# Gated cross-attention walks: order of VectorE's inverse and first addition, and of four maximum products on TensorE

## The chip, the cores and the metric

The program runs on one core of one Trainium2 chip. A core has TensorE (matmuls; PE in the profile, with its weight loads as PEld), VectorE (DVE), ScalarE (ACT), GpSimd (POOL) and SyncE (SP, which issues the DMAs here). Each engine works through its own instructions in order, and semaphores tie the engines together. The metric is the device time of one execution in microseconds (us).

## The reference

Four layers on x (16 sequences of 56 tokens, 256 features) with a context of 1500 rows of 128 features for each sequence. The first is self attention, cross attention and a gated feed-forward, the second a cross attention with a memory gate. The third and fourth are alike, and only their attention is touched here:

```
q = layernorm(x) @ Wq * scale                    # 16 heads of 64
k, v = split(media @ Wkv)                        # media: the context
sim = einsum('bhid,bhjd->bhij', q, k)
sim = where(media_mask[:, None, None, :], sim, neg_inf)
attn = softmax(sim)
x = x + tanh(attn_gate) * (attn @ v merged over heads @ Wo)
x = x + tanh(ff_gate) * (gelu(layernorm(x) @ W1) @ W2)
```

The mask handed in is true only for context positions beyond a sequence's length, so that `where` leaves no more than the last 375 of a sequence's 1500 rows: one chunk. The kernel's code has a second path for sequences with more than one chunk (`several`), which these inputs do not take.

## The kernel before

For each of the two gated layers (`l` 0 and 1) a walk over the batch handles one sequence after the other: B = 16 walks, written out one by one in the path taken. Queries are folded with the key weights, so that scores are products against the context itself: 896 columns (16 heads x 56 tokens) by 375 context rows. Walk b does two things at once.

It finishes sequence b from turned scores. `turned(u)`, u = 0 to 5, is a set of four matmuls (L2395 to L2398) for a third of the 375 rows and a half of the 896 columns; three multiply queries and context in split precision, the fourth subtracts the maxima by way of a diagonal matrix. ScalarE takes the exponential of each (`exps`, L1174, tile WA), and `values(u)` (L2403) multiplies it with the context into PSUM banks 5 and 6. VectorE adds the three thirds of the exponentials in `add_tiles` (L1727, the first addition) and `add_last` (L1733, the last addition).

It prepares sequence b + 1. `behind(j)`, j = 0 to 7, calls `maxima` (product at L2375) for one pair of heads into bank j % 2; `masked_maximum` on VectorE (L1710) adds the mask and takes the row maximum. In the trace it is two records, CUSTOM_DVE_ANT_0 and DVE_READ_ACCUMULATOR2_ANT. A product j waits until maximum j - 2 has read its bank (`x2_rowmax`). After the eighth maximum GpSimd builds the diagonal matrix (`diagonal`, L812, tile XN), for which `turned(0)` of the next walk waits. GpSimd then prepares a later context (`keys`, L803, L805, L807).

The denominators belong to the sequence before: in walk b, `denominators` on TensorE (L2411) multiplies the added exponentials of sequence b - 1 with ones into bank 7. VectorE copies them out (`denominators`, L1717) and inverts them in two halves (`invert(b, 0)` and `invert(b, 1)`, both L1723). The first exponential of a walk waits for the last addition of the walk before (`x2_dsum`), since it overwrites what that reads; the first addition waits for the fourth exponential, the last for the sixth.

The order on each engine is the order in which the code of `batch` (VectorE), `step` (TensorE, ScalarE) is written.

Of the kernel before, what the change touches and what calls it, by code (L numbers as in the profile page):

```python
# [198 lines left out]
def build(nc, a, out):  # L199

    ctx = ExitStack()
    with ctx:
# [1019 lines left out]
        def _(dve):  # L1222
# [250 lines left out]
            def invert(b):  # L1473

                dve.wait_ge(sem("z_one_each"), b + 1)
                V.reciprocal(z_few[:, 1, :], z_few[:, 1, :]).then_inc(sem("z_inverted"), 1)
# [218 lines left out]
            for l in range(2):  # L1695
                queries(l, 0, {0: lambda: centre("nq", l, 1), 3: lambda: inverse_root("nq", l, 1, 0),
                               4: lambda: inverse_root("nq", l, 1, 1), 5: lambda: scale("nq", l, 1, 0, 1)})
                queries(l, 1, {})

                def maximum(b, p, j):  # L1700
                    wait_at(dve, "x2_scores", PAIRS * (l * B + b) + j + 1)
                    V.tensor_reduce(y_max[p][0:PR, j:j + 1], bank[j % 2][0:PR, 0:CK], AX_X, ALU.max)\
                        .then_inc(sem("x2_rowmax"), 1)

                def masked_maximum(b, s, j):

                    if j == 0:
                        dve.wait_ge(sem(f"x2_mask{s}"), 16 * (B // SLOTS * l + b // SLOTS + 1 - (l + 1) * (s == 0)))
                    dve.wait_ge(sem("x2_scores"), PAIRS * (l * B + b) + j + 1)
                    V.tensor_tensor_reduce(y_masked[0:PR, j % 2, 0:CK], bank[j % 2][0:PR, 0:CK], y_mask[0:PR, s, 0:CK], 1.0, -3e38,  # L1710
                                           ALU.add, ALU.max, y_max[s % 2][0:PR, j:j + 1])\
                        .then_inc(sem("x2_rowmax"), 1)

                def denominators(k):

                    wait_at(dve, "x2_dn", l * (B + 1) + k + 1)
                    V.tensor_copy(y_den[:, bass.ds(k, 1), :].rearrange("p b n -> p (b n)"), bank[7][:, 0:HALF])\  # L1717
                        .then_inc(sem("x2_den"), 1)
                    wait_at(dve, "x2_den", l * (B + 1) + k + 2)

                def invert(k, g):
                    part = y_den[:, bass.ds(k, 1), g * HALF // 2:(g + 1) * HALF // 2].rearrange("p b n -> p (b n)")
                    V.reciprocal(part, part).then_inc(sem("x2_inverted"), 1)  # L1723

                def add_tiles(b):
                    wait_at(dve, "x2_expd", PARTS * (l * B + b) + 4 + 3)
                    V.tensor_tensor(y_sum[0:TK, :], y_pT[0][0:TK, :], y_pT[1][0:TK, :], ALU.add)\  # L1727
                        .then_inc(sem("x2_dsum"), 1)

                def add_last(b):  # L1730
                    wait_at(dve, "x2_expd", PARTS * (l * B + b) + PARTS + 3)
                    wait_at(dve, "x2_dsum", 2 * (l * B + b) + 3)
                    V.tensor_tensor(y_sum[0:TK, :], y_sum[0:TK, :], y_pT[2][0:TK, :], ALU.add)\  # L1733
                        .then_inc(sem("x2_dsum"), 1)

                def batch(b, s, nxt, nxt2, nxt3, several):
                    p = s % 2
                    for j in range(PAIRS):
                        if nxt and several:
                            maximum(b + 1, 1 - p, j)  # L1740
                        elif nxt:
                            masked_maximum(b + 1, (s + 1) % SLOTS, j)
                        if j == 2:
                            denominators(b)
                            invert(b, 0)
                        if j == 5:
                            add_tiles(b)
                    invert(b, 1)
                    add_last(b)

                    def extra(x, i):
                        old = y_max[p]
                        for j in range(PAIRS):
                            extra_step(dve, x, 4 + 2 * j)
                            V.tensor_reduce(y_low[0:PR, j:j + 1], bank[j % 2][0:PR, 0:CK], AX_X, ALU.max)\
                                .then_inc(sem("x2_extra"), 1)
                        extra_step(dve, x, 19)
                        V.tensor_tensor(y_new[0:PR, :], y_low[0:PR, :], old[0:PR, :], ALU.max).then_inc(sem("x2_extra"), 1)
                        extra_step(dve, x, 20)
                        V.tensor_tensor(y_step[0:PR, :], old[0:PR, :], y_new[0:PR, :], ALU.subtract)\  # L1760
                            .then_inc(sem("x2_extra"), 1)
                        extra_step(dve, x, 21)
                        V.tensor_copy(old[0:PR, :], y_new[0:PR, :]).then_inc(sem("x2_extra"), 1)
                        extra_step(dve, x, 26)
                        for g in range(2):
                            half_g = slice(g * HALF, (g + 1) * HALF)
                            V.tensor_copy(y_wide[:, half_g], bank[2 + g][:, 0:HALF])
                            last = V.tensor_tensor(y_sum[0:TK, half_g], y_sum[0:TK, half_g], bank[2 + g][0:TK, 0:HALF],
                                                   ALU.mult)
                        last.then_inc(sem("x2_extra"), 1)  # L1770
                        extra_step(dve, x, 27)
                        for g in range(2):
                            half_g = slice(g * HALF, (g + 1) * HALF)
                            last = V.tensor_tensor(y_sofar[:, half_g], bank[5 + g][:, 0:HALF], y_wide[:, half_g], ALU.mult)
                        last.then_inc(sem("x2_extra"), 1)
                        extra_step(dve, x, 46)
                        for g in range(2):
                            V.tensor_tensor(bank[5 + g][:, 0:HALF], bank[5 + g][:, 0:HALF],
                                            y_sofar[:, g * HALF:(g + 1) * HALF], ALU.add)
                        for t in range(KT):  # L1780
                            V.tensor_tensor(y_sum[0:TK, :], y_sum[0:TK, :], y_pT[t][0:TK, :], ALU.add)\
                                .then_inc(sem("x2_extra"), 1)
                            extra_step(dve, x, 47 + t)

                    if several:
                        over_extras(dve, l, b, more, extra)

                for j in range(PAIRS):
                    maximum(0, 0, j)
                walks(dve, more, batch)  # L1790
                denominators(B)
                for g in range(2):
                    invert(B, g)
                projected(l, 0, {})
                projected(l, 1, {1: lambda: centre("nf", l, 0), 4: lambda: inverse_root("nf", l, 0, 0),
                                 5: lambda: inverse_root("nf", l, 0, 1), 6: lambda: scale("nf", l, 0, 2, 3)})
                norm("nf", l, 1, 2, 3)
                fed_forward(l, 0)
                if l == 0:
                    norm("nq", 1, 0, 0, 1)  # L1800
                fed_forward(l, 1)
# [3 lines left out]
        def _(pe):  # L1805
# [561 lines left out]
            for l in range(2):  # L2367
# [48 lines left out]
                def step(b, s, nxt, nxt2, nxt3, several):  # L2416
# [5 lines left out]
                    def behind(j):  # L2422
                        if nxt:
                            maxima(b + 1, (s + 1) % SLOTS, c, j)

                    def turned(u):
                        if u == 0:
                            wait_at(pe, "x2_diag", l * B + b + 1)
                        wait_at(pe, "x2_expd", at + u + 1)
                        turned_scores(b, s, u).then_inc(sem("x2_st"), 1)  # L2430

                    def values(u):
                        wait_at(pe, "x2_expd", at + u + 4)
                        if u < 2:

                            wait_at(pe, "x2_out", 2 * (l * B + b) + u + 1)
                        attended(s, u).then_inc(sem("x2_pv"), 1)
# [7 lines left out]
                    denominators(b)  # L2445
                    behind(3)
                    turned(2)
                    behind(4)
                    values(1)
                    behind(5)  # L2450
                    turned(3)
                    behind(6)
                    values(2)
                    behind(7)
                    turned(4)
                    values(3)
                    turned(5)
                    values(4)
# [84 lines left out]
```

## Time and profile before

| | |
|---|---|
| time, median of 3 runs | 1589.75 us (1589.52 to 1590.13) |
| profiled execution, its own time | 1590.39 us |
| profiled execution, span from first to last instruction | 1588.6 us |
| TensorE busy | 1473.9 us, 93% |
| VectorE busy | 946.9 us, 60% |
| ScalarE busy | 621.6 us, 39% |
| GpSimd busy | 539.5 us, 34% |
| mean granted TensorE clock | 0.983 |
| masked walks, first layer | from 907.54 us, about 204 us |
| masked walks, second layer | from 1277.57 us, about 203 us |

The span is the time between the first and the last instruction of the program in one profiled execution. In the trace, matmuls are pipelined: a matmul's record lasts longer than the time until the next one can start, so what a matmul costs TensorE is read from start to start. A float32 matmul such as L2403 appears as two records. "Idle before" is the time in which an engine had nothing running ahead of an instruction, and the name behind the arrow is what ended it.

### The profile page before, as it was taken

To read this page: it belongs to the slowest core of one execution; us is meant where nothing else is said; L and a number is where in the kernel's file an instruction comes from. 1 tells how busy PE (TensorE), PEld (TensorE's weight loads), DVE (VectorE), ACT (ScalarE), POOL (GpSimd) and SP (SyncE) were. 2 spreads that over 40 slices of the span, in tenths; PEclk is the share of its full clock that TensorE was granted. 3 is DMA by queue.
4 is the path that set the end of the run, shared out by engine and by line. 5 is a ranking of instruction groups with operands and counts; after the bars stand their busy time and mean duration, and the time that the engine had idled before them with its cause. 6 is when DMAs were issued, how large, how long until landed. Compare 5 with 4: busy or idle time off the path is not lost.

```text
span 1588.6 us, 21924 instructions
## 1 busy us (share of the span) xinstructions
PE 1473.9 (93%) x8042; PEld 780.1 (49%) x8043; DVE 946.9 (60%) x1605; ACT 621.6 (39%) x1014; POOL 539.5 (34%) x425
## 2 busy tenths in 40 slices
PE   7889999999999799989988899999999889999998
PEld 3346555555555454456654354554344345554344
DVE  6887666666666163123437577777343767777440
ACT  1253566666666521035542333334122333333131
POOL 1710688888888900000001133332000133333000
PEclk9989999999999999989999899999999999999999
DMA  7001523233232040023211011110031001110000
GB/s 254 1 5 47 145 74 98 60 89 79 69 98 52 9 138 0 0 78 117 77 34 65 0 35 37 36 36 2 2 112 65 0 24 36 36 36 13 2 0 23
DMA packets 42276, 82.96 MB, mean 52 GB/s; under 512 B 6252, under 2 KB 28188, under 8 KB 42156
## 3 DMA queue, kind: packets, MB, share of 16 engines
q1 hardware_dynamic: 42160, 81.48, 17.7%
q8 instruction: 65, 1.06, 0.3%
q14 instruction: 51, 0.42, 0.1%
HBM read 59.31 MB, written 0.97 MB: 38 GB/s over the span
## 4 chain that ended last, share of the span: by engine, by line
PE 79%; DVE 13%; POOL 3%; issue 2%; ACT 2%; DMA 0%; SPq 0%; POOLq 0%; ACTq 0%; DVEq 0%
PE psum L1820 21%; PE psum L2403 8%; PE psum L2061 5%; PE psum L2037 5%; PE psum L2011 4%; PE psum L2344 3%; DVE WBZ L1723 3%; PE psum L1994 3%; PE psum L2211 3%; PE psum L1980 2%; POOL XN L780 2%; PE psum L2375 2%; DVE WA L1463 2%; PE psum L2411 2%; PE psum L2395 2%
## 5 line engine op out<-in xcount | busy, mean ns | idle before, releaser
L1463 DVE TENSOR_REDUCE WA<-psum 112x2 f32<-112x1000 f32 x192 | 229.8, 1200 | 89.9 <-PE psum L2011 89.9
L780 POOL TENSOR_TENSOR XN<-XN,WBZ 125x896 f32<-125x896 f32 x128 | 266.4, 2082 | 16.8 <-POOL XN L780 0.9
L1174 ACT ACTIVATE WA<-psum,y_bias 125x448 f32<-125x448 f32 x192 | 121.1, 633 | 228.0 <-PE psum L2398 227.0
L1008 ACT ACTIVATE WBZ<-psum 125x896 f32<-125x896 f32 x192 | 175.5, 915 | 43.9 <-PE psum L2037 33.7
L2403 PE MATMUL psum<-WA,ctxN 125*128 125x448 f32 x384 | 180.1, 552 | 0.4 <-ACT WA L1174 0.4
L812 POOL TENSOR_TENSOR XN<-const,y_max 112x896 bf16<-112x896 f32 x32 | 53.7, 1679 | 309.3 <-DVE y_max L1710 237.0
L1710 DVE CUSTOM_DVE_ANT_0 XA<-psum,WA 112x375 bf16<-112x375 f32 x240 | 122.6, 540 | 35.1 <-PE psum L2375 35.1
L803 POOL TENSOR_SCALAR ctxT<-ctxT 128x375 f32<-128x375 f32 x32 | 56.1, 1754 | 190.5 <-ACT std L881 188.0
L2037 PE MATMUL psum<-R 100*125 100x224 f16 x768 | 110.7, 266 | 0.0
L1723 DVE RECIPROCAL WBZ<-WBZ 128x224 f32<-128x224 f32 x68 | 105.1, 1548 | 1.2
L2375 PE MATMUL psum<-XB,R 128*112 128x375 f16 x240 | 77.5, 343 | 22.7 <-DVE y_max L1710 22.7
L2037 PEld LDWEIGHTS psum<-R 100*125 100x125 f16 x768 | 78.9, 135 | 28.3 <-issue 25.0
L1820 PE MATMUL psum<-R,WBZ 128*128 128x448 f32 x224 | 88.5, 548 | 2.5 <-ACT R L886 2.5
L2403 PEld LDWEIGHTS psum<-WA,ctxN 125*128 125x128 f32 x384 | 67.3, 191 | 31.9 <-ACT WA L1174 24.5
L2011 PE MATMUL psum<-WA,XB 32*112 32x500 f16 x384 | 79.3, 413 | 2.5 <-DVE WA L1463 2.3
L1820 PE MATMUL psum<-XA,WA 64*128 64x448 f32 (+1 forms) x216 | 72.5, 573 | 2.1 <-DVE XA L1644 1.9
L2395 PE MATMUL psum<-R,XB 128*125 128x448 f16 x192 | 68.5, 357 | 4.9 <-POOL XN L812 4.9
L2375 PEld LDWEIGHTS psum<-XB,R 128*112 128x112 f16 x240 | 31.5, 131 | 84.2 <-DVE y_max L1710 69.6
L2398 PE MATMUL psum<-XN,minusb 112*125 112x448 bf16 x192 | 68.7, 358 | 0.0
L2397 PE MATMUL psum<-R,XB 128*125 128x448 f16 x192 | 68.3, 356 | 0.0
L2396 PE MATMUL psum<-R,XB 128*125 128x448 f16 x192 | 68.1, 355 | 0.0
L1820 PEld LDWEIGHTS psum<-R,WBZ 128*128 128x128 f32 x224 | 40.9, 189 | 50.1 <-issue 44.7
(266 smaller groups left out, 2565.3 us busy)
## 6 DMA issues: line engine op xcount, KB each, us to landing
R<-WA SPq DMA_DIRECT2D x192, 93.8 KB, 2.2
ctxT<-in_ctxT SPq DMA_DIRECT2D x12, 750.0 KB, 4.3
R<-in_ctxT SPq DMA_DIRECT2D x12, 750.0 KB, 5.4
WA<-in_ctxT SPq DMA_DIRECT2D x8, 750.0 KB, 4.1
ctxT<-in_ctxT SPq DMA_DIRECT2D x32, 187.5 KB
ctxN<-in_ctx SPq DMA_DIRECT2D x32, 187.5 KB
WBZ<-in_x_w SPq DMA_DIRECT2D x4, 1024.0 KB, 6.5
WA<-bias_rows SPq DMA_DIRECT2D x30, 82.0 KB, 3.6
```

Source lines behind the costliest of these rows:

```text
L780: nc.gpsimd.tensor_tensor(z_sum[b % 2][0:TK, :], first[0:TK, :], z_p[t % 4][0:TK, :], ALU.add)\
L1008: nc.scalar.activation(z_p[t % 4][0:TK, :].rearrange("p (k n) -> p k n", k=2), psum[0:TK, s:s + 2, 0:2 * GC], ACT.Exp, scale=float(CHD0) * ...
L1174: nc.scalar.activation(y_pT[t][0:TK, g * HALF:(g + 1) * HALF], bank[2 + u % 3][0:TK, 0:HALF], ACT.Exp, bias=y_bias[0:TK, bass.ds(b * NT + ...
L1463: V.tensor_reduce(z_mx[0:PR, r:r + 3:2, c], psum[0:PR, lo:lo + 2, 0:PC], AX_X, ALU.max)\
L1710: V.tensor_tensor_reduce(y_masked[0:PR, j % 2, 0:CK], bank[j % 2][0:PR, 0:CK], y_mask[0:PR, s, 0:CK], 1.0, -3e38, ALU.add, ALU.max, y_max[ ...
L1723: V.reciprocal(part, part).then_inc(sem("x2_inverted"), 1)
L1820: mm = pe.matmul(bank[bk][0:w.shape[-1], 0:HT], w, m, start=(i == 0), stop=(i == len(parts) - 1))
L2011: mm = pe.matmul(bank[lo + j][0:PR, 0:PC], z_dh[at, b, 2 * (i % 2):2 * (i % 2) + 2, :].rearrange("p h s -> p (h s)"), z_kh[b % 2][at, c * ...
L2037: mm = pe.matmul(bank[2 * (t % 2) + g // 2][0:TK, g % 2 * GC:(g % 2 + 1) * GC], KS[0:KR, b % 2, g, t * TK:(t + 1) * TK], QS[0:KR, g, b, :] ...
L2375: return pe.matmul(bank[j % 2][0:PR, 0:CK], y_q[:, b, 0, j * PR:(j + 1) * PR], y_k[:, s, 0, 0:CK], start=True, stop=True)
L2395: pe.matmul(dst, y_k[:, s, 0, at], q[0], start=True, stop=False)
L2403: return pe.matmul(bank[5 + g][:, 0:HALF], ctxN[s][0:TK, t, :], y_pT[t][0:TK, g * HALF:(g + 1) * HALF], start=(t == 0), stop=(t == KT - 1))
```

## The change

In `batch` on VectorE the first inverse moves from behind the third to behind the fourth maximum, and the first addition from behind the sixth to behind the eighth. In `step` on TensorE the value products and turned scores between `behind(3)` and `values(3)` change places with `behind(4)` to `behind(7)`, so that each of these four comes one place later.

```
@@ -1742,9 +1742,9 @@
                             masked_maximum(b + 1, (s + 1) % SLOTS, j)
                         if j == 2:
                             denominators(b)
+                        if j == 3:
                             invert(b, 0)
-                        if j == 5:
-                            add_tiles(b)
+                    add_tiles(b)
                     invert(b, 1)
                     add_last(b)
 
@@ -2445,14 +2445,14 @@
                     denominators(b)
                     behind(3)
                     turned(2)
+                    values(1)
                     behind(4)
-                    values(1)
+                    turned(3)
                     behind(5)
-                    turned(3)
+                    values(2)
                     behind(6)
-                    values(2)
+                    turned(4)
                     behind(7)
-                    turned(4)
                     values(3)
                     turned(5)
                     values(4)
```

The orders of ScalarE, GpSimd and SP stay as they are. On TensorE, in a masked walk behind `turned(2)`, there stands before (L2375 is a maximum product, L2403 a value product, L2395 to L2398 a set of turned scores):

```order
L2375 MATMUL psum<-XB,R 112x375
L2403 MATMUL psum<-WA,ctxN 128x448
L2375 MATMUL psum<-XB,R 112x375
L2395 MATMUL psum<-R,XB 125x448
L2396 MATMUL psum<-R,XB 125x448
L2397 MATMUL psum<-R,XB 125x448
L2398 MATMUL psum<-XN,minusb 125x448
L2375 MATMUL psum<-XB,R 112x375
L2403 MATMUL psum<-WA,ctxN 128x448
L2375 MATMUL psum<-XB,R 112x375
```

and in the changed kernel, at the same place:

```order
L2403 MATMUL psum<-WA,ctxN 128x448
L2375 MATMUL psum<-XB,R 112x375
L2395 MATMUL psum<-R,XB 125x448
L2396 MATMUL psum<-R,XB 125x448
L2397 MATMUL psum<-R,XB 125x448
L2398 MATMUL psum<-XN,minusb 125x448
L2375 MATMUL psum<-XB,R 112x375
L2403 MATMUL psum<-WA,ctxN 128x448
L2375 MATMUL psum<-XB,R 112x375
```

The four products L2375 are the fifth to the eighth; in the changed kernel the eighth follows one more set of turned scores behind the last row shown.

On VectorE, behind the third maximum of a masked walk (L1717 copies the denominators, L1723 is the first inverse, a pair of L1710 rows is one maximum), before:

```order
L1717 COPY WBZ<-psum 128x448
L1723 RECIPROCAL WBZ<-WBZ 128x224
L1710 ISA XA,y_max<-psum,WA 112x375
L1710 ISA y_max 112x1
L1710 ISA XA,y_max<-psum,WA 112x375
```

and in the changed kernel:

```order
L1717 COPY WBZ<-psum 128x448
L1710 ISA XA,y_max<-psum,WA 112x375
L1710 ISA y_max 112x1
L1723 RECIPROCAL WBZ<-WBZ 128x224
L1710 ISA XA,y_max<-psum,WA 112x375
```

The inverse now stands behind the fourth maximum.

On VectorE at the end of the same walk, from the first addition (L1727) on, before:

```order
L1727 TENSOR_TENSOR WA<-WA 125x896
L1710 ISA XA,y_max<-psum,WA 112x375
L1710 ISA y_max 112x1
L1710 ISA XA,y_max<-psum,WA 112x375
L1710 ISA y_max 112x1
L1723 RECIPROCAL WBZ<-WBZ 128x224
L1733 TENSOR_TENSOR WA<-WA 125x896
```

and in the changed kernel, from the eighth maximum on:

```order
L1710 ISA XA,y_max<-psum,WA 112x375
L1710 ISA y_max 112x1
L1727 TENSOR_TENSOR WA<-WA 125x896
L1723 RECIPROCAL WBZ<-WBZ 128x224
L1733 TENSOR_TENSOR WA<-WA 125x896
```

The first addition, the second inverse and the last addition now follow the eighth maximum in a row.

## Rows read from the trace of the kernel before

**Rows 1.** Stretch: length, PE, PEld, DVE, ACT, POOL busy (records), clock, DMA, GB/s

```profile
907.54:1111.70 204.16, 192.14 (x760) 102.13 (x760) 155.74 (x320) 79.14 (x129) 70.13 (x57) 0.99 0.10 29
```

**Rows 2.** Costliest groups, maximum products: count, busy, mean ns, idle before, releaser

```profile
L2375 PE MATMUL psum<-XB,R 128*112 128x375 f16 x240 | 77.5, 343 | 22.7 <-DVE y_max L1710 22.7
```

**Rows 3.** Timeline, TensorE, ninth walk: start, duration (us), instruction, [idle before]

```profile
1011.65 0.35 PE L2395 MATMUL psum<-R,XB 128*125 128x448 f16 x1
...
1012.41 0.32 PE L2375 MATMUL psum<-XB,R 128*112 128x375 f16 x1
...
1013.70 0.92 PE L2403 MATMUL psum<-WA,ctxN 125*128 125x448 f32 x2
...
1015.45 0.37 PE L2375 MATMUL psum<-XB,R 128*112 128x375 f16 x1
...
1016.41 0.32 PE L2375 MATMUL psum<-XB,R 128*112 128x375 f16 x1
1016.58 0.92 PE L2403 MATMUL psum<-WA,ctxN 125*128 125x448 f32 x2
1018.25 0.37 PE L2375 MATMUL psum<-XB,R 128*112 128x375 f16 x1 [0.75 <-DVE y_max L1710]
1018.45 0.35 PE L2395 MATMUL psum<-R,XB 128*125 128x448 f16 x1
...
1019.37 0.92 PE L2403 MATMUL psum<-WA,ctxN 125*128 125x448 f32 x2
1020.12 0.32 PE L2375 MATMUL psum<-XB,R 128*112 128x375 f16 x1
...
1021.80 0.35 PE L2395 MATMUL psum<-R,XB 128*125 128x448 f16 x1
...
1022.56 1.91 PE L2403 MATMUL psum<-WA,ctxN 125*128 125x448 f32 x4
1024.30 0.35 PE L2395 MATMUL psum<-R,XB 128*125 128x448 f16 x1
```

**Rows 4.** Timeline, VectorE, the same walk

```profile
1012.88 0.55 DVE L1710 CUSTOM_DVE_ANT_0 XA<-psum,WA 112x375 bf16<-112x375 f32 x1 [0.66 <-PE psum L2375]
...
1015.57 0.62 DVE L1717 COPY WBZ<-psum 128x448 f32<-128x448 f32 x1 [0.85 <-PE psum L2411]
...
1017.69 0.49 DVE L1710 CUSTOM_DVE_ANT_0 XA<-psum,WA 112x375 bf16<-112x375 f32 x1
...
1020.07 1.09 DVE L1727 TENSOR_TENSOR WA<-WA 125x896 f32<-125x896 f32 x1 [0.86 <-ACT WA L1174]
1021.08 0.54 DVE L1710 CUSTOM_DVE_ANT_0 XA<-psum,WA 112x375 bf16<-112x375 f32 x1
...
1021.55 0.55 DVE L1710 CUSTOM_DVE_ANT_0 XA<-psum,WA 112x375 bf16<-112x375 f32 x1
...
1022.02 1.55 DVE L1723 RECIPROCAL WBZ<-WBZ 128x224 f32<-128x224 f32 x1
1023.48 1.39 DVE L1733 TENSOR_TENSOR WA<-WA 125x896 f32<-125x896 f32 x1
```

**Rows 5.** Timeline, ScalarE, the same walk: first two and sixth exponential

```profile
1012.86 1.30 ACT L1174 ACTIVATE WA<-psum,y_bias 125x448 f32<-125x448 f32 x2 [0.47 <-PE psum L2398]
...
1022.76 0.63 ACT L1174 ACTIVATE WA<-psum,y_bias 125x448 f32<-125x448 f32 x1 [0.78 <-PE psum L2398]
```

**Rows 6.** Timeline, GpSimd, the same walk: diagonal and the keys behind it

```profile
1022.25 1.68 POOL L812 TENSOR_TENSOR XN<-const,y_max 112x896 bf16<-112x896 f32 x1 [7.50 <-DVE y_max L1710]
1024.01 1.89 POOL L803 TENSOR_SCALAR ctxT<-ctxT 128x375 f32<-128x375 f32 x1
```

**Rows 7.** Timeline, all engines, start of the first walk

```profile
905.81 1.68 POOL L812 TENSOR_TENSOR XN<-const,y_max 112x896 bf16<-112x896 f32 x1 [36.08 <-DVE y_max L1702]
...
907.54 0.63 PE L2395 MATMUL psum<-R,XB 128*125 128x448 f16 x1 [2.46 <-POOL XN L812]
907.57 1.17 POOL L803 TENSOR_SCALAR ctxT<-ctxT 128x375 f32<-128x375 f32 x1
```

More of the change, by code:

```diff
@@ L1744, in batch @@
                             denominators(b)
+                        if j == 3:
                             invert(b, 0)
-                        if j == 5:
-                            add_tiles(b)
+                    add_tiles(b)
                     invert(b, 1)
@@ L2447, in step @@
                     turned(2)
+                    values(1)
                     behind(4)
-                    values(1)
+                    turned(3)
                     behind(5)
-                    turned(3)
+                    values(2)
                     behind(6)
-                    values(2)
+                    turned(4)
                     behind(7)
-                    turned(4)
                     values(3)
```

## Prediction

> **What bounds the kernel now.** The change touches only the gated walks, two stretches of some 204 us with 16 walks each, so I first asked what one walk waits for there. I read the costliest groups, then the busy times of one stretch, then the timelines of TensorE, VectorE, ScalarE and GpSimd over the ninth walk of the first stretch, which stands for its neighbours. Names used below: T0 to T5 are the score sets of four matmuls (L2395 to L2398), M0 to M7 the maximum products of the next walk (L2375), max0 to max7 their maxima on VectorE (L1710 with its read-out), V0 to V5 the value products (L2403), D the denominators (L2411), exp0 to exp5 the exponentials (L1174), the diagonal is GpSimd's L812, the two inverses are L1723, the first addition is L1727 and the last L1733. Times are us from the T0 of the walk.
>
> TensorE is the busy engine: 192.1 of 204.2 us, at a mean granted clock of 0.99 [rows 1]. The group of M products carries 22.7 us of TensorE's idle time, released by y_max [rows 2]. The timeline places it: V1 stands at 1016.58, M5 at 1018.25 with 0.75 us idle before it [rows 3]. M5 reuses the PSUM bank of M3, so it needs max3, and max3 (1017.69) stands behind the copy of D (1015.57) and the first inverse [rows 4]. 22.7/0.75 = 30 stalls: one for each walk that has a next one, 15 in each stretch. A walk lasts 1024.30 - 1011.65 = 12.65 us [rows 3].
>
> **The change part by part.** Nothing is added or removed in the taken path: three DVE steps and four PE products a walk change places. ScalarE, GpSimd and SP keep their orders. So the sum is a new schedule of one walk, made from measured intervals.
>
> Intervals between starts on PE: a T set 1022.56 - 1021.80 = 0.76; an M 1016.58 - 1016.41 = 0.16 (0.17 by rounding); a V 1020.12 - 1019.37 = 0.75; V0 stands at 2.05, M3 at 3.80 and T2 0.20 later (as T3 behind M5), at 4.00 [rows 3]. On DVE: a maximum takes the place of 0.47 (two in 1022.02 - 1021.08), an addition 1.01 (1021.08 - 1020.07), an inverse 1.46 (1023.48 - 1022.02), the copy of D 0.66 (it starts 1015.57, and max3, one inverse later, 1017.69); a maximum starts 0.47 after its product (1012.41, which is T0 + 0.76, to 1012.88) and releases PE 0.62 after its start (0.56 with the read-out, then 0.06; after the inverse 1017.69 to 1018.25, 0.56) [rows 3, 4].
>
> *PE's new order.* Up to T2 nothing moves. Then V1 at 4.76, M4 5.52, T3 5.68, M5 6.44, V2 6.60, M6 7.36, T4 7.52, M7 8.28, V3 8.44, T5 9.19, V4 9.95. V5 needs exp5, which starts 1022.76 - 1021.80 = 0.96 after T5 and takes 0.63 [rows 3, 5]: V5 at 9.19 + 0.96 + 0.63 + 0.05 (the release) = 10.83, as it waits today. Today V5 so stands 0.88 behind V4 and the next T0 1.74 behind V4: V5 takes 0.86 [rows 3]. PE could thus start the next T0 at **11.69**. exp1 to exp4 are done at least 0.8 us before their V, by the same 0.96 + 0.63 behind their T.
>
> *First inverse behind max3.* Copy of D at 3.92, max3 at 4.58, inverse at 5.05, max4 at 6.51. M5 needs max3: 4.58 + 0.62 = 5.20, it stands at 6.44, so the 0.75 us stall **goes**. Late next is M6, which needs max4: 6.51 + 0.56 = 7.07 against 7.36, a margin of only 0.29. If it were gone, each 0.1 us would cost 0.1 x 30 = 3 us. M7 needs max5 (6.92, releasing at 7.54) against 8.28.
>
> *First addition behind max7.* Before, it stood in front of max6 and waited for exp3 (0.86 idle) [rows 4]. Now max6 and max7 follow their products: max6 at 7.83, max7 at 8.75, against 1021.55 - 1011.65 = 9.90 now. The diagonal starts 1022.25 - 1021.55 = 0.70 after max7 [rows 4, 6], hence at 9.45, and takes 1.68: done at 11.13 if undisturbed, before PE wants it at 11.69.
>
> *What stands in its way.* The addition now starts at 8.75 + 0.47 = 9.22, 0.23 before the diagonal, where an inverse stood before. The trace shows what two such operations do to each other. L1733 starts at 1023.48 while the diagonal runs until 1023.93, and takes 1.39 where L1727, of the same shape, takes 1.09 alone: overlap 0.45, cost 0.30. L803 starts at 1024.01 while L1733 holds until 1024.87, and takes 1.89 instead of 1.17: overlap 0.86, cost 0.72. So the later one pays the overlap less about 0.14 [rows 4, 6, 7]. The inverses cost nobody anything: the diagonal takes 1.68 beside one and 1.68 in the first walk, with VectorE idle [rows 6, 7]. The rows thus show one operation blocking the other, not both slowed. I take the addition as first: it runs 9.22 to 10.31, overlaps the diagonal by 0.86 and costs it 0.72. The diagonal ends at 11.13 + 0.72 = **11.85**. In the first walk PE started T0 0.05 after the diagonal's end (907.49 to 907.54) [rows 7], and a matmul after an idle wait takes 0.20 instead of 0.16 to the next [rows 3]. The next T0 then stands effectively at 11.85 + 0.05 + 0.04 = **11.94**.
>
> The Trainium skill, page "SBUF — State Buffer", section "SBUF: two separate sides", says that the SBUF port pair which VectorE and GpSimd share is an exclusive lock for the whole instruction and that whichever starts first has it. By that rule the trace agrees in both directions, except that a blocked instruction still hides some 0.14 us of its start. The same page's later section on bandwidth pools gives a blocked transfer as waiting until VectorE's end plus about 115 ns. By an estimate from that figure the diagonal would run its full 1.68 from 10.42, the walk would be 12.19 and the time 1576; L803's cost of 0.72 for an overlap of 0.86 speaks against it.
>
> *The tail on VectorE.* Second inverse at 10.23, last addition at 11.69 (the diagonal ends at 11.85, whose remaining 0.16 is about what is hidden), done at 12.8. The next exp0 waits for it and for the next T0 (11.94 + 1.21 = 13.15, from 1012.86 - 1011.65) [rows 3, 5]: no cost. The next max0 wants VectorE at 13.17, free at 12.7: no cost. L803 is blocked by the last addition as it is today; nothing waits for it before the following walk. No DMA is moved.
>
> **Sum.** 12.65 - 11.94 = 0.71 us a walk, x 30 = 21.3 us. First and last walks: the first has the same stall; the last has no M and gains nothing of its own. Profiled span 1588.6 becomes 1567.3; the median 1589.75 becomes **1568.4**. Bounds of the only unseen price, the addition beside the diagonal: nothing for either engine gives 11.78 (the last addition then takes 1.39 and holds the next max0 and exp0 back by 0.09), a gain of 0.87 x 30 = 26.1; 0.30 paid by the addition, none by the diagonal, gives 12.08, a gain of 17.1. I take the blocked diagonal, since the addition starts 0.23 us earlier and since L803 behind L1733 is the nearest row.
>
> **Rivals.**
> 1. *No loss at the diagonal.* PE or the DVE tail bounds the walk at 11.69 to 11.78: 1589.75 - 26 to 29 = 1561 to 1564. For it: neither pair of operations has met in this order. Against it: both directions of the cost are in the trace. 0.12.
> 2. *VectorE pays a little, or M6 waits.* The addition takes 1.39, and the last one and exp0 come 0.30 later still than at 11.78: walk 12.08, time 1572.6. For it: the margin of 0.29 at M6 and +0.30 as the only surcharge that VectorE shows here. 0.15. The estimate by the Trainium skill's 115 ns lies beyond it, at 1576.
> 3. *Slower: the diagonal blocks the addition.* The place is the 0.23 us between the two starts; it happens when the addition, though issued first, takes hold later than the diagonal does. Then the diagonal ends at 11.13, the addition at 11.13 + 1.09 - 0.14 = 12.08, the second inverse starts at 12.00, the last addition at 13.46 and ends at 14.55. The next exp0 runs to 15.24, and the next V0 stands at 15.29 instead of T0 + 2.05: a walk of 13.24, longer by 0.59, x 30 = 17.7: 1607.4. For it: two additions and an inverse now follow max7, and exp0 waits for all. Against it: 0.23 us of lead. 0.07. By the Trainium skill's rule of the exclusive lock, the order of the two starts is exactly what decides.
> 4. *The change does not do what it says, no net change.* The stall only moves (to M6 or T0) in full: 1589 to 1590. It would need 0.75 us of new wait; I find 0.25 at T0. 0.03.
>
> The forecast itself gets 0.63. Beside all of them, stretches at the lower clock level (the first T0 takes 0.63 where others take 0.35 [rows 3, 7]) can fall a few us elsewhere; I give that 2 us either way.
>
> **How the numbers follow.** A measurement of this kernel can tell about 0.2% (3.2 us) from no change. Faster: 0.63 + 0.12 + 0.15 = 0.90; same 0.03; slower 0.07. The forecast's own range is 1566 to 1571. The 80% range takes in the bounds 1563.6 and 1572.6 with 2 us of clock: 1561.5 to 1574.5; outside are rivals 3 and 4, the far end of rival 2, and what I have not seen.
>
> **What would show it.** Right: no idle time at M5; the walk 11.9; the diagonal near 2.4 us long, starting 0.23 after the first addition, which stays at 1.09; the last addition near 1.1 instead of 1.39; PE's weight load of T0 waiting for the diagonal. Wrong: a diagonal of 1.68 (rival 1 or 3, told apart by the addition's length: 1.09 or near 2.9), idle time at M6, or V0 waiting for exp0.

## Result, and the profile after

| | before | changed |
|---|---|---|
| time, median | 1589.94 us (1589.52 to 1590.33) | 1563.97 us (1562.47 to 1566.13) |
| ratio | | 0.9838, 95% interval 0.9821 to 0.9855 |
| profiled span | 1588.6 us | 1562.6 us |

The change saves 26 us, 1.6%. The forecast was 1568.4 with a range of 1561.5 to 1574.5. A second measurement of the changed kernel, beside the experiments below, gave 1564.14 and a ratio of 0.984 (0.9824 to 0.9857).

The page of the changed kernel, costliest groups: count, busy us, mean ns, idle before and its releaser. The maximum products (compare [rows 2]) show no idle time any more, and the diagonal L812 takes 2350 ns in the mean (the first of each stretch still takes 1.68 us, the others 2.39 to 2.40).

```profile
L812 POOL TENSOR_TENSOR XN<-const,y_max 112x896 bf16<-112x896 f32 x32 | 75.2, 2350 | 263.9 <-DVE y_max L1710 191.6
...
L2375 PE MATMUL psum<-XB,R 128*112 128x375 f16 x240 | 76.1, 337 | 0.0
```

Busy times of the changed kernel by stretch, columns as in [rows 1]: the first masked stretch from its first turned scores on, and one walk.

```profile
907.60:1099.50 191.90, 191.19 (x760) 102.08 (x760) 151.63 (x320) 79.17 (x129) 80.86 (x57) 0.98 0.11 30
1005.10:1016.93 11.83, 11.83 (x49) 6.37 (x48) 9.72 (x22) 4.89 (x8) 5.63 (x4) 1.00 0.14 40
```

In the first row TensorE is busy for 191.2 of 191.9 us, where it was 192.1 of 204.2 [rows 1]: the work is the same and the idle time is gone. The second row shows a walk without any in the records; a wait can still lie under a matmul's modelled end, as the weight load below shows.

The timeline of TensorE in the ninth walk of the changed kernel (start, duration, instruction), which answers to [rows 3]:

```profile
1005.10 0.40 PE L2395 MATMUL psum<-R,XB 128*125 128x448 f16 x1
...
1009.91 0.92 PE L2403 MATMUL psum<-WA,ctxN 125*128 125x448 f32 x2
1010.67 0.32 PE L2375 MATMUL psum<-XB,R 128*112 128x375 f16 x1
...
1011.59 0.32 PE L2375 MATMUL psum<-XB,R 128*112 128x375 f16 x1
...
1012.50 0.32 PE L2375 MATMUL psum<-XB,R 128*112 128x375 f16 x1
...
1013.42 0.32 PE L2375 MATMUL psum<-XB,R 128*112 128x375 f16 x1
...
1016.93 0.40 PE L2395 MATMUL psum<-R,XB 128*125 128x448 f16 x1
```

V1 and M4 to M7 follow each other at the distances of the plan (M4 at 5.57, M5 6.49, M6 7.40, M7 8.32 of the walk), and the next T0 comes after 11.83 us instead of 12.65.

VectorE in the same walk (answers to [rows 4]): the copy of the denominators, fourth maximum, first inverse, then the eighth maximum, first addition, second inverse, last addition.

```profile
1009.07 0.62 DVE L1717 COPY WBZ<-psum 128x448 f32<-128x448 f32 x1 [0.84 <-PE psum L2411]
...
1009.73 0.55 DVE L1710 CUSTOM_DVE_ANT_0 XA<-psum,WA 112x375 bf16<-112x375 f32 x1
...
1010.20 1.55 DVE L1723 RECIPROCAL WBZ<-WBZ 128x224 f32<-128x224 f32 x1
...
1013.78 0.55 DVE L1710 CUSTOM_DVE_ANT_0 XA<-psum,WA 112x375 bf16<-112x375 f32 x1 [0.36 <-PE psum L2375]
...
1014.26 1.09 DVE L1727 TENSOR_TENSOR WA<-WA 125x896 f32<-125x896 f32 x1
1015.26 1.55 DVE L1723 RECIPROCAL WBZ<-WBZ 128x224 f32<-128x224 f32 x1
1016.72 1.11 DVE L1733 TENSOR_TENSOR WA<-WA 125x896 f32<-125x896 f32 x1
```

GpSimd in the same walk (answers to [rows 6]):

```profile
1014.49 2.39 POOL L812 TENSOR_TENSOR XN<-const,y_max 112x896 bf16<-112x896 f32 x1 [5.97 <-DVE y_max L1710]
1016.97 1.89 POOL L803 TENSOR_SCALAR ctxT<-ctxT 128x375 f32<-128x375 f32 x1
```

And the weight load of the next T0:

```profile
1016.93 0.13 PEld L2395 LDWEIGHTS psum<-R,XB 128*125 128x125 f16 x1 [0.65 <-POOL XN L812]
```

The first addition starts at 1014.26 and holds until 1015.35, the diagonal starts at 1014.49 and takes 2.39 instead of 1.68, and TensorE starts the next T0 0.05 after its end (1016.88). TensorE shows no idle time there, because the modelled end of V5 reaches that far; it is the weight load's wait that tells.

### The profile page after: what moved, and what is told of

Same layout as the page of the kernel before. It is cut to its first block, busy times and chain, and to the rows that moved or that the text cites. A ratio compares the mean times of both kernels' runs of the same rounds, so it can differ in the third digit from the quotient of the medians.

```text
span 1562.6 us, 21954 instructions
## 1 busy us (share of the span) xinstructions
PE 1470.6 (94%) x8042; PEld 779.7 (50%) x8043; DVE 939.1 (60%) x1605; ACT 621.7 (40%) x1014; POOL 561.0 (36%) x425
## 3 DMA queue, kind: packets, MB, share of 16 engines
q8 instruction: 65, 1.06, 0.3%
## 4 chain that ended last, share of the span: by engine, by line
PE 85%; DVE 8%; POOL 2%; ACT 2%; issue 2%; DMA 0%; SPq 0%; POOLq 0%; ACTq 0%; DVEq 0%
PE psum L1820 22%; PE psum L2403 10%; PE psum L2061 5%; PE psum L2037 5%; PE psum L2011 4%; PE psum L2344 3%; PE psum L1994 3%; PE psum L2375 3%; PE psum L2211 3%; PE psum L2395 3%; PE psum L1980 2%; PE psum L2398 2%; PE psum L2396 2%; PE psum L2397 2%; DVE WA L1463 2%
## 5 line engine op out<-in xcount | busy, mean ns | idle before, releaser
L2403 PE MATMUL psum<-WA,ctxN 125*128 125x448 f32 x384 | 179.5, 551 | 0.4 <-ACT WA L1174 0.4
L812 POOL TENSOR_TENSOR XN<-const,y_max 112x896 bf16<-112x896 f32 x32 | 75.2, 2350 | 263.9 <-DVE y_max L1710 191.6
L1710 DVE CUSTOM_DVE_ANT_0 XA<-psum,WA 112x375 bf16<-112x375 f32 x240 | 125.4, 542 | 47.1 <-PE psum L2375 46.0
L803 POOL TENSOR_SCALAR ctxT<-ctxT 128x375 f32<-128x375 f32 x32 | 56.1, 1754 | 189.7 <-ACT std L881 187.1
L1723 DVE RECIPROCAL WBZ<-WBZ 128x224 f32<-128x224 f32 x68 | 105.0, 1546 | 0.1
L2403 PEld LDWEIGHTS psum<-WA,ctxN 125*128 125x128 f32 x384 | 67.1, 190 | 31.7 <-ACT WA L1174 24.4
L2375 PE MATMUL psum<-XB,R 128*112 128x375 f16 x240 | 76.1, 337 | 0.0
L2395 PE MATMUL psum<-R,XB 128*125 128x448 f16 x192 | 70.0, 365 | 4.9 <-POOL XN L812 4.9
L2398 PE MATMUL psum<-XN,minusb 112*125 112x448 bf16 x192 | 68.9, 359 | 0.0
L2396 PE MATMUL psum<-R,XB 128*125 128x448 f16 x192 | 68.4, 356 | 0.0
L890 ACT ACTIVATE R<-psum 128x448 f16<-128x448 f32 x64 | 31.3, 543 | 79.2 <-PE psum L1820 79.2
```

What stands on the lines that cost most here:

```text
L2375: return pe.matmul(bank[j % 2][0:PR, 0:CK], y_q[:, b, 0, j * PR:(j + 1) * PR], y_k[:, s, 0, 0:CK], start=True, stop=True)
L2395: pe.matmul(dst, y_k[:, s, 0, at], q[0], start=True, stop=False)
L2403: return pe.matmul(bank[5 + g][:, 0:HALF], ctxN[s][0:TK, t, :], y_pT[t][0:TK, g * HALF:(g + 1) * HALF], start=(t == 0), stop=(t == KT - 1))
```

## Experiments

Walks below are from T0 to T0 in the trace, in the ninth walk of the first stretch unless another is named. With 30 walks that have a next one, 0.1 us of a walk is 3 us of the total. The lines of the programs shift by one to three where an experiment adds lines, so L2375, L2395, L2403 can stand as L2376, L2396, L2404.

| kernel | walk, us | median, us | ratio to before (95%) |
|---|---|---|---|
| before | 12.65 | 1589.9 | |
| changed | 11.83 | 1563.97 | 0.9838 (0.9821 to 0.9855) |
| changed, once more | 11.83 | 1564.1 | 0.9840 (0.9824 to 0.9857) |
| first inverse moved alone | 12.20 | 1576.3 | 0.9914 (0.9898 to 0.9931) |
| TensorE's order alone | 11.89 | 1566.0 | 0.9848 (0.9831 to 0.9864) |
| changed, addition behind the 6th maximum | 11.69 | 1561.2 | 0.9817 (0.9797 to 0.9837) |
| changed, addition behind the 7th | 11.69 | 1561.5 | 0.9815 (0.9799 to 0.9832) |
| changed, second inverse ahead of the additions | 12.36 | 1580.3 | 0.9938 (0.9921 to 0.9955) |
| changed, first addition in halves | 13.38 | 1612.6 | 1.0148 (1.0129 to 1.0167) |
| addition behind the 6th, T5 earlier | 11.45 | 1548.6 | 0.9743 (0.9726 to 0.9760) |
| the same once more | 11.45 | 1551.8 | 0.9764 (0.9748 to 0.9780) |
| addition behind the 8th, T5 earlier | 11.83 | 1562.1 | 0.9826 (0.9809 to 0.9842) |
| addition behind the 7th, one reciprocal added | 11.96 | 1569.3 | 0.9869 (0.9847 to 0.9890) |
| the same, two reciprocals added | 12.42 | 1583.3 | 0.9957 (0.9941 to 0.9974) |

### The parts alone

First inverse alone, against the kernel before:

```
                             denominators(b)
+                        if j == 3:
                             invert(b, 0)
```

> Only the first inverse moves, behind the fourth maximum; TensorE and the first addition keep their old places. Theory A (each stall is bound by the maximum two places before it, and the schedule of one walk adds up): the 0.75 us in front of M5 go, but M6 then stands at 6.61 us and needs the fifth maximum, which releases it at 7.07: part of the stall moves to M6. Walk 12.20 instead of 12.65 us, total 1576.4 us. Rival B (the inverse was the whole cause, and TensorE's new order adds nothing): no idle time at any maximum product, walk 11.7 to 11.8, total 1563 to 1564.

Measured: walk 12.20, total 1576.3. TensorE's timeline, M4, M5 and M6 of this kernel:

```profile
1011.70 0.32 PE L2376 MATMUL psum<-XB,R 128*112 128x375 f16 x1
...
1012.61 0.32 PE L2376 MATMUL psum<-XB,R 128*112 128x375 f16 x1
...
1014.00 0.37 PE L2376 MATMUL psum<-XB,R 128*112 128x375 f16 x1 [0.30 <-DVE y_max L1710]
```

The walk starts at 1006.93. M4 (1011.70) stands where it did, M5 (1012.61, 5.68 of the walk) no longer waits, and M6 stands still until 7.07, as worked out. The inverse was not the whole cause: with TensorE's old order the stall moves one product on, and the walk regains 0.45 of the 0.96 us that lie between 12.65 and TensorE's own 11.69.

TensorE's order alone: the lines of the change in `step`, with `batch` as before.

> Only TensorE's order changes; VectorE keeps its old one. Theory A: M5 stands at 6.44 and is released by the fourth maximum at 6.60, so 0.16 us of the stall stay, and the first addition, still behind the sixth maximum, lets the diagonal run undisturbed (1.68 us). Walk 11.89 us, total 1567.0 us. Rival B: the stall stays at 0.75 us, since the inverse has not moved; walk 12.6, total about 1589.

Measured: walk 11.89, total 1566.0. M5 starts 6.60 after its T0, and the group of maximum products shows no idle time:

```profile
L2375 PE MATMUL psum<-XB,R 128*112 128x375 f16 x240 | 77.4, 343 | 0.0
```

The 0.16 us that M5 still waits lie under the modelled end of T3. So TensorE's order alone brings nearly all of the gain, 1.5% of 1.6%; the two moves on VectorE together add 0.06 us a walk. The next runs split these 0.06: the inverse's move gives 0.20 (11.89 to 11.69), and the addition's takes 0.14 of it back (11.69 to 11.83).

### The first addition's place

In the changed kernel:

```
-                    add_tiles(b)
+                        if j == 5:
+                            add_tiles(b)
```

> The changed kernel with the first addition back behind the sixth maximum. Theory A (in the changed kernel the walk is bound by the diagonal, which the addition blocks): the diagonal takes 1.68 instead of 2.40 us and ends before TensorE is through, the walk is TensorE's own 11.69 to 11.72 us, total 1560 to 1561 us, 3 to 4 us under the changed kernel. Rival C (the addition's move is part of the gain, since the seventh and eighth maximum no longer stand behind it): walk 11.9 or more, total 1566 or more.

and the same with `j == 6`:

> The changed kernel with the first addition between the seventh and the eighth maximum. Theory A: the addition runs 8.2 to 9.3 us, the diagonal starts at 9.94 after it, takes 1.68 and ends at 11.62, just before TensorE is through at 11.69: walk 11.69 to 11.74, total 1560 to 1562 us. Rival D (what counts is only when the eighth maximum is done, 0.56 us later here than in the changed kernel): walk 12.3 to 12.4, total about 1580.

Measured: both 11.69, totals 1561.2 and 1561.5. The diagonal in the timeline of the first (its T0 is 1005.35, the next 1017.04):

```profile
1012.74 1.08 DVE L1727 TENSOR_TENSOR WA<-WA 125x896 f32<-125x896 f32 x1
...
1014.91 1.68 POOL L812 TENSOR_TENSOR XN<-const,y_max 112x896 bf16<-112x896 f32 x1 [6.54 <-DVE y_max L1710]
```

and of the second (T0 1004.01, the next 1015.70):

```profile
1012.19 1.09 DVE L1727 TENSOR_TENSOR WA<-WA 125x896 f32<-125x896 f32 x1
...
1013.89 1.68 POOL L812 TENSOR_TENSOR XN<-const,y_max 112x896 bf16<-112x896 f32 x1 [6.54 <-DVE y_max L1710]
```

The diagonal starts later in both than in the changed kernel (9.56 and 9.88 of the walk against 9.39), and yet it ends earlier, at 11.24 and 11.56 against 11.78, since no addition stands beside it. The moved addition thus costs the change 0.14 us a walk, about 4 us; the totals differ by 2 to 3 us, which their intervals do not separate, but the walks do. Rivals C and D are out.

### Who blocks whom

Second inverse ahead of the first addition:

```
-                    add_tiles(b)
                     invert(b, 1)
+                    add_tiles(b)
                     add_last(b)
```

> The changed kernel with the second inverse ahead of the first addition. Theory A (one of the two engines blocks the other): the diagonal meets only the inverse and takes 1.68 us; the addition starts at 10.61, is blocked until 11.06 and takes 1.40; GpSimd's L803 waits meanwhile and runs next, since the last addition must wait for the first one's end; the last addition is blocked by it for about a microsecond, ends at about 14.0, and the next first exponential waits: walk about 12.7 us, total about 1590, all of the gain gone. Rival E (both engines are slowed in proportion, nobody waits for the other's end): last addition done by 13.2, walk 11.7 to 11.9, total 1561 to 1567.

Timeline, VectorE and GpSimd, from the second inverse on (T0 is 1008.86, the next 1021.22):

```profile
1018.64 1.55 DVE L1723 RECIPROCAL WBZ<-WBZ 128x224 f32<-128x224 f32 x1
1018.87 1.68 POOL L812 TENSOR_TENSOR XN<-const,y_max 112x896 bf16<-112x896 f32 x1 [7.14 <-DVE y_max L1710]
...
1020.11 1.39 DVE L1727 TENSOR_TENSOR WA<-WA 125x896 f32<-125x896 f32 x1
...
1020.63 1.89 POOL L803 TENSOR_SCALAR ctxT<-ctxT 128x375 f32<-128x375 f32 x1
...
1021.60 1.20 DVE L1733 TENSOR_TENSOR WA<-WA 125x896 f32<-125x896 f32 x1
```

The first three steps came as theory A says: diagonal 1.68, addition blocked until its end (1.39), L803 blocked by the addition (1.89). The fourth did not: the last addition runs for 0.92 us beside L803 and loses 0.11 (1.20 instead of 1.09), not 0.8. So the walk is 12.36, not 12.7. Theory A was wrong about L803 as a blocker. Rival E has no blocked addition and a walk of 11.9 at most, so it is out.

First addition in halves:

```
-V.tensor_tensor(y_sum[0:TK, :], y_pT[0][0:TK, :], y_pT[1][0:TK, :], ALU.add)\
+V.tensor_tensor(y_sum[0:TK, 0:HALF], y_pT[0][0:TK, 0:HALF], y_pT[1][0:TK, 0:HALF], ALU.add)
+V.tensor_tensor(y_sum[0:TK, HALF:], y_pT[0][0:TK, HALF:], y_pT[1][0:TK, HALF:], ALU.add)\
     .then_inc(sem("x2_dsum"), 1)
```

> The changed kernel with the first addition as two instructions of 448 columns each, issued without a wait between them. Theory A, if GpSimd gets its turn between the two: the diagonal is blocked only by the first half and takes about 1.9 us; the second half is blocked until its end, the second inverse, last addition and next first exponential come late: walk about 12.9 us, total about 1598, slower than before. Theory A, if VectorE keeps its turn: diagonal about 2.5, walk 11.9 to 12.0, total 1566 to 1569. Rival E (shared in proportion): as the changed kernel plus the 0.1 us that one more instruction takes, diagonal 2.4 to 2.5, both halves lengthened a little.

Timeline, VectorE, GpSimd and the two engines that wait, from the first half on (tenth T0 1028.66):

```profile
1026.08 0.62 DVE L1727 TENSOR_TENSOR WA<-WA 125x448 f32<-125x448 f32 x1
...
1026.30 1.93 POOL L812 TENSOR_TENSOR XN<-const,y_max 112x896 bf16<-112x896 f32 x1 [7.73 <-DVE y_max L1710]
...
1026.61 2.10 DVE L1728 TENSOR_TENSOR WA<-WA 125x448 f32<-125x448 f32 x1
...
1031.61 1.16 ACT L1174 ACTIVATE WA<-psum,y_bias 125x448 f32<-125x448 f32 x2 [2.20 <-DVE WA L1734]
...
1031.77 0.37 PE L2376 MATMUL psum<-XB,R 128*112 128x375 f16 x1 [1.10 <-DVE y_max L1710]
```

GpSimd gets its turn between the halves. The diagonal pays for the first half (overlap 0.39, cost 0.25), then the second half, 0.62 long, takes 2.10 (overlap 1.62, cost 1.48). Everything behind it on VectorE is late: M2 of the next walk waits 1.10 for max0, the exponentials wait 2.20 for the last addition. The walk is 13.38, 0.73 longer than before the change, and the total 1612.6, slower than before. This is the slower rival of the prediction, its mechanism set going: the same work, cut in two, costs 1.55 us a walk more than in one piece. I had expected 12.9. What was left out: an exponential released by the last addition starts 0.36 after its end (1031.25 to 1031.61), where I had counted 0.05, and the value product behind it restarts some 0.1 slower, as V5 does. These two make up 0.41 of the 0.48 us. The distance of 0.36 is the same in the three other kernels in which the last addition ends too late for the exponential (the run above, 1022.80 to 1023.16, and the two of the last section). Both are paid only where ScalarE waits for VectorE, so they touch neither the kernel before nor the changed one.

### The next bound

Addition behind the sixth maximum, and on TensorE T5 earlier:

```
                     behind(7)
+                    turned(5)
                     values(3)
-                    turned(5)
                     values(4)
```

> Addition back behind the sixth maximum, and on TensorE the last turned scores T5 one place earlier, ahead of V3, so that the sixth exponential is done before V5 wants it. Theory A: TensorE's own time is 11.69 with 0.13 us of waiting at V5 and some 0.1 of restart in it; without them 11.47. The diagonal ends at 11.25, the last addition at 12.2, both early enough: walk 11.47 us, total 1554 to 1555 us, better than both kernels. Rival: the walk stays at 11.7 (another wait takes its place), total 1561.

The same T5 with the addition behind the eighth maximum:

> The same earlier T5, but with the first addition behind the eighth maximum as in the changed kernel. Theory A (the blocked diagonal bounds the walk there): TensorE is through at 11.47 and waits for the diagonal, which still ends at 11.78: walk 11.83 us, total 1564 us, no gain over the changed kernel, and 0.3 us of idle time in front of the first turned scores. Rival (TensorE's own time or V5's wait bounds the changed kernel): walk 11.5 to 11.6, total 1555 to 1557.

Measured: 11.45 and 11.83. In the second kernel TensorE now shows its wait for the diagonal openly (timeline, GpSimd and TensorE):

```profile
1012.76 2.40 POOL L812 TENSOR_TENSOR XN<-const,y_max 112x896 bf16<-112x896 f32 x1 [5.96 <-DVE y_max L1710]
...
1015.22 0.40 PE L2395 MATMUL psum<-R,XB 128*125 128x448 f16 x1 [0.17 <-POOL XN L812]
```

With T5 earlier, TensorE has 0.24 us less to do or wait for (11.69 to 11.45), and in the second kernel not a hundredth of it reaches the walk. That pins the changed kernel's bound: its 11.83 are the blocked diagonal and nothing else. The first kernel takes 2.6% less than the kernel before, in the second measurement 2.4%, where the changed one takes 1.6% less.

> The kernel with the addition behind the sixth maximum and the earlier T5 once more. Walks of 11.45 us. If the 5 us beyond its walks belong to the kernel, the total is again 1548 to 1550 with a granted clock of 0.988; if they were chance of the clock, it is 1551 to 1555 with 0.984.

Measured: walks of 11.45 again, median 1551.8. Its four executions show a granted clock of 0.988, 0.986, 0.981 and 0.981 at 1548.3, 1551.7, 1551.9 and 1553.4 us, where the first measurement had 0.987 to 0.988 throughout. So one and the same kernel takes 3 to 5 us more where the granted clock is lower, and the gain of some 5 us beyond its walks in the first measurement was in large part chance; the two medians lie about 1550. The traces show the same from another side: up to the first masked walk all kernels are alike, and yet it starts anywhere from 905.2 to 908.9 us in their profiled executions.

> The changed kernel once more, on the same chip as the two beside it. Walks of 11.83 us as before. If the part of the total that the walks do not explain (1.4 us here, 5 us in the run with the earlier T5) is chance of the clock's lower stretches on one chip, the total lies within 1562 to 1566 and that remainder moves by a few us.

Measured: walks of 11.83, 1564.14 us, clock 0.983 to 0.986.

### When an operation takes hold

To see why L803 hardly blocked, one reciprocal of constants was put ahead of the last addition of the kernel with the addition behind the seventh maximum, then a second one:

```
                     invert(b, 1)
+                    V.reciprocal(XA[0:PR, 1, 400:512], ones[0:PR, 0:112])
+                    V.reciprocal(XA[0:PR, 0, 0:72], ones[0:PR, 0:72])      # second run only
                     add_last(b)
```

> The kernel of the run with the first addition behind the seventh maximum, plus one reciprocal of 112 constants into unused space between the second inverse and the last addition (about 0.8 us on VectorE). It puts the start of the last addition at about 11.85 us of the walk, inside L803, GpSimd's one-input multiplication, which starts undisturbed at 11.65 and alone would end at 12.82. Theory A (whichever starts first blocks the other, whatever its kind): the last addition takes about 1.9 us, the next first exponential comes late, walk 12.4 to 12.5, total about 1584. Theory F (a one-input GpSimd operation does not block VectorE's addition, as in the run with the second inverse first, where an overlap of 0.93 cost the addition 0.10): the last addition takes about 1.2 us, walk 11.7 to 11.8, total about 1562.

Timeline, first of the two:

```profile
1018.68 2.23 POOL L803 TENSOR_SCALAR ctxT<-ctxT 128x375 f32<-128x375 f32 x1
1018.86 1.03 DVE L1733 TENSOR_TENSOR WA<-WA 125x896 f32<-125x896 f32 x1
```

The addition starts 0.18 after L803 and loses nothing: all 32 of these additions take 1.02 to 1.03 in this run and 1.03 in the next, the last two of each as well, beside which no L803 runs (why 1.03 here and 1.09 elsewhere, I do not know). L803 pays 1.06 for an overlap of 1.03. Neither theory foresaw that: A had the addition at 1.9, and F had nothing that would stretch L803. The order of the records' starts does not decide for this pair, then: L803 had not taken hold 0.18 us after its record starts. (The profile's spans on GpSimd are rough, so the 0.18 is as good as its records.) Walk 11.96, total 1569.3, where F had 11.7 to 11.8 and about 1562; the next exponential waits for the addition and starts the 0.36 us later that the run with the halves has shown.

> As the run with one extra reciprocal of constants ahead of the last addition, with a second one of 72 columns behind it. There the addition started only 0.18 us after L803, was not delayed at all (1.03 us), and L803 was stretched to 2.23: GpSimd had not taken hold yet. Now the last addition starts some 0.6 us after an undisturbed L803, which alone takes 1.17. Theory A (an operation holds to its end, once it has taken hold): the addition is blocked for the rest of L803 and takes about 1.5 us, L803 stays at 1.17; walk about 12.8, total about 1594. Theory F (a one-input GpSimd operation holds only briefly, which the 0.10 us of the run with the second inverse first suggest): the addition takes 1.1 to 1.2 and L803 1.2; walk 12.3 to 12.5, total 1580 to 1586. Theory G (GpSimd is always set aside): the addition takes 1.03 to 1.09 and L803 about 2.2; walk 12.3 to 12.4.

Timeline, second of the two:

```profile
1020.07 1.17 POOL L803 TENSOR_SCALAR ctxT<-ctxT 128x375 f32<-128x375 f32 x1
...
1020.71 1.03 DVE L1733 TENSOR_TENSOR WA<-WA 125x896 f32<-125x896 f32 x1
1021.30 0.79 POOL L805 CAST XB<-ctxT 128x375 f16<-128x375 f32 x1
```

Starting 0.64 after L803, the addition loses nothing, and L803 neither, with 0.53 us side by side. The cast behind it, which starts while the addition runs, pays (0.79 instead of 0.50). Walk 12.42, total 1583.3. Theory A is out for L803, G too. F comes nearest: if this one-input operation holds at all, then for a short time only. Whether it does at a point between 0.18 and 0.64 us, and how long, stays open, and so does why the two-input L812 holds to its end.

## Why the prediction was right

**Where the stall was and that it goes.** Right. The 22.7 us at M5 are gone, and no later product waits. M6, named as next with a margin of 0.29 us, has kept it: in the changed kernel max4 is done 7.05 after T0 (1011.66 + 0.49), the weight load of M6 is released at 7.11, and M6 stands at 7.40. The run with the inverse alone shows what M6 does without TensorE's new order (0.30 idle, and 0.46 late).

**The diagonal.** Right in sign, cause and size. Forecast: addition at 9.22 for 1.09, diagonal from 9.45 to 11.85, 2.40 long. Measured: 9.16 for 1.09, 9.39 to 11.78, 2.39 long. The runs with the addition at other places show that it is this meeting that sets the walk. The term "less about 0.14" held in the experiments too, at 0.08 to 0.15 in every pair but those in which L803 stood ahead of an addition. There it did not: ahead by 0.18, L803 itself paid, with nothing taken off (1.03 of overlap cost 1.06); ahead by more, the addition paid 0.11 for 0.92 and nothing for 0.53.

**The sum.** 0.71 us a walk forecast, 0.82 measured. The term that was off is "a maximum starts 0.47 after its product". That was max0's distance, and it is 0.47 in the changed kernel too. The eighth maximum followed its product by 0.36 (1013.42 to 1013.78), the seventh as well; the kernel before had shown 0.36 for M1, a row that I did not take. In the code max0 alone has a second wait ahead of it, for the mask (`x2_mask`); whether that makes the 0.11, no run shows. The shorter distance brings the diagonal forward by 0.11. The 0.04 that the restart of T0 costs fall at the walk's beginning and not, as I had put them, at its end, so the diagonal starts only about 0.07 earlier than forecast, and the walk is 0.11 shorter. 0.11 x 30 = 3.3 of the 4.4 us between forecast and result. The rest, 26.0 less 30 x 0.82 = 24.6, lies outside the walks; the measurements at different granted clocks above make chance of the clock likely, as the 2 us either way had allowed. The result keeps to the 80% range, but not to the forecast's own 1566 to 1571: it is 2 us under it.

**The tail on VectorE.** Right: last addition 1.11 instead of 1.39, next max0 with 0.39 idle before it, L803 still 1.89.

**The bounds.** One step in the bound of 11.78 has no source: it gives the last addition its 1.39, though a diagonal done at 11.13 no longer stands beside an addition that starts at 11.69. Without it that bound is 11.69, 2.7 us of the total lower, and still within rival 1.

**The rivals.** The result, 1564.0, stands at the edge of rival 1 (1561 to 1564), but its mechanism did not happen: the diagonal was blocked. The walk of 11.69 that it named is what the two runs with the addition elsewhere reach. The slower rival did not happen: the addition led by 0.23 us. If L812 took hold as late after its record's start as L803 (more than 0.18 us), that rival was further off than I priced it, but no run shows this for L812. What set it off was the cut: with the diagonal waiting through the first half, GpSimd came in ahead of the second.

**What I did not ask.** Whether each part of the change helps. The first addition's move loses 0.14 us a walk; my own figures (diagonal undisturbed at 11.13, TensorE through at 11.69) held the better kernel already.

## What to carry to other kernels

When an engine waits for a step that stands late on another, try moving the waiting work later as well as moving the blocking step: here the first alone (TensorE's four products) gave 1.5%, the second alone (the inverse) 0.9%, and all moves together 1.6%. A schedule of one period, made from start-to-start intervals, gave the walk to 0.11 us or better in the changed kernel and in the six experiments whose waits were all in the rows; where a wait came in that no row had shown, it was off by up to 0.5. Take each interval from a row of the same place or kind. A two-input addition on VectorE and the two-input L812 on GpSimd run one behind the other here: put the addition where GpSimd is not on the path, here ahead of the last maximum, and do not cut it into pieces there, as the other engine comes in between. Before accepting a change of several moves, undo each alone.

## What the runs showed of the hardware

- Additions with two inputs on VectorE and GpSimd's two-input L812 run one after the other: the one that starts second pays the overlap less about 0.14 us, in both directions (0.45 costs 0.30; 0.86 costs 0.72; 1.62 costs 1.48). Of this pair the Trainium skill's page "SBUF — State Buffer", section "SBUF: two separate sides", holds: a lock, for the whole instruction.
- For the one-input L803 that rule holds only one way. It is blocked by an addition (1.89 and 2.23 instead of 1.17), but an addition that starts 0.64 after it runs undisturbed beside it, and one that starts 0.10 after L803 was let go loses 0.11 for an overlap of 0.92. Here the measurement differs from the page, and the measurement decides.
- L803, whose record starts 0.18 us before an addition's, still loses to it, and pays 1.06 us.
- Two halves of an addition, issued without a wait between them, let the waiting L812 in between: the second half took 2.10 us instead of 0.62.
- The reciprocals, with one input, cost GpSimd nothing: L812 takes 1.68 and L803 1.17 beside them.
- The first exponential starts 0.36 us after the last addition's end, in each of the four runs in which that addition comes too late for it; TensorE's T0 starts 0.05 us after the diagonal's end.
